# One sum with the shared expert in front, in place of two sums joined at the end

## What is computed

```python
scores = sigmoid(x @ router_w.T)                      # 4096 tokens, 16 experts
_, topk_idx = top_k(scores + e_bias, 4)
topk_w = take(scores, topk_idx) / sum                 # 4 experts for each token
...
for each expert: acc += combine[:, e] * ((silu(g) * u) @ d_w.T)    # I = 192, H = 512
shared = (silu(x @ shared_gate_w.T) * (x @ shared_up_w.T)) @ shared_down_w.T
return x2 + routed + shared
```

## Time and profile before

| | |
|---|---|
| median of 3 runs | 1870.16 us (1867.11 to 1880.34) |
| profiled execution, its own time | 1878.89 us |
| its span, first to last instruction | 1877.1 us |
| mean granted TensorE clock | 0.980 |
| busy, share of span | TensorE 95%, VectorE 61%, GpSimd 49%, ScalarE 47% |

### The profile page before, as it was taken

The page is one execution under the profiler, slowest core; times in us unless marked ns, Lnnn a source line. Parts: engine busy times, 40 slices in busy tenths (PEclk is TensorE's granted clock), DMA queues, the critical chain, the costliest instruction groups (busy, mean ns, idle before and its releaser), DMA issues. The chain is left out here.

```text
span 1877.1 us, 35163 instructions
## 1 busy us (share of the span) xinstructions
PE 1784.7 (95%) x8536; PEld 901.2 (48%) x8537; DVE 1145.0 (61%) x2171; ACT 880.2 (47%) x1726; POOL 924.6 (49%) x1127
## 2 busy tenths in 40 slices
PE   6799999999999999999999889899999999999995
PEld 5444454444454444544433345455555555555542
DVE  5567778787878787787788726433343333343433
ACT  2257766776676767667776642122211222211210
POOL 3424546676676667666555356033333333333341
PEclk9799999999999999999999989999999999999998
DMA  5422325344344534453345279898898888898889
GB/s 192 117 75 54 87 81 154 93 115 139 103 119 124 156 99 107 129 143 85 105 136 168 99 236 352 255 198 154 160 168 161 157 159 158 161 167 159 163 178 254
DMA packets 255899, 277.76 MB, mean 148 GB/s; under 512 B 57889, under 2 KB 184097, under 8 KB 253025
## 3 DMA queue, kind: packets, MB, share of 16 engines
q0 software_dynamic: 40880, 106.96, 27.1%
q1 hardware_dynamic: 151600, 127.10, 25.3%
q10 hardware_dynamic: 63296, 42.24, 8.3%
HBM read 145.65 MB, written 135.74 MB: 150 GB/s over the span
## 5 line engine op out<-in xcount | busy, mean ns | idle before, releaser
L995 DVE TENSOR_REDUCE mx<-ps_max 128x2 f32<-128x1024 f32 x512 | 618.3, 1220 | 175.3 <-PE ps_max L1205 160.5
L734 ACT ACTIVATE prob<-ps_exp 128x512 f32<-128x512 f32 x992 | 567.5, 598 | 147.9 <-PE ps_exp L1219 129.9
L1977 PE MATMUL ps_gu<-wts_sb,xT 128*128 x1152 | 399.4, 490 | 1.3 <-issue 1.3
L1219 PE MATMUL ps_exp<-qs,ks 98*128 98x512 bf16 x992 | 379.2, 383 | 19.0 <-ACT prob L734 16.6
L1205 PE MATMUL ps_max<-ks,qs 96*128 96x512 bf16 x1024 | 309.5, 384 | 10.7 <-DMA ks<-qk_parts 6.1
L1728 ACT ACTIVATE gs<-ps_gu 128x192 f32<-128x192 f32 x176 | 58.4, 332 | 520.1 <-PE ps_gu L1977 258.4
L1977 PEld LDWEIGHTS ps_gu<-wts_sb,xT 128*128 128x128 f32 x1152 | 209.7, 190 | 161.6 <-issue 46.5
L1676 POOL DMA_INDIRECT out<-yt,idx x72 | 111.7, 1551 | 355.5 <-ACT yt L1738 272.7
L1247 PE MATMUL ps_pv<-prob,vs 128*32 128x512 f32 x2048 | 252.8, 607 | 2.9 <-issue 2.9
L1219 PEld LDWEIGHTS ps_exp<-qs,ks 98*128 98x128 bf16 x992 | 96.7, 97 | 195.2 <-ACT prob L734 82.4
L1886 DVE SCALAR_TENSOR_TENSOR hid<-ps_gu,wsel,gs 128x192 f32<-128x192 f32 (+2 forms) x216 | 68.4, 345 | 173.4 <-ACT gs L1728 133.1
(11 more groups left out here) (196 smaller groups left out, 1997.6 us busy)
## 6 DMA issues: line engine op xcount, KB each, us to landing
xt<-rows_by_expert SPq DMA_DIRECT2D x296, 64.0 KB
dnr_sb<-in_dnr SPq DMA_DIRECT2D x144, 128.0 KB
xt<-rows_by_expert ACTq DMA_DIRECT2D x280, 64.0 KB
qk_parts<-parts POOLq DMA_DIRECT2D x112, 120.0 KB, 3.7
qs<-qk_parts SPq DMA_DIRECT2D x64, 192.0 KB, 3.1
wts_sb<-in_wts ACTq DMA_DIRECT2D x12, 1024.0 KB, 8.2
x_sb<-in_x SPq DMA_DIRECT2D x16, 512.0 KB
qs<-qk_parts SPq DMA_DIRECT2D x64, 128.0 KB, 3.2
```

The lines of the kernel that those rows point to most:

```text
L734: act.activation(prob[:, s, q], ps_exp[:, q % 2], ACT.Exp, scale=SCALE).then_inc(s_exp, 1)
L995: dve.tensor_reduce(mx[:, k % 2, 4 * s + 2 * p:4 * s + 2 * p + 2], ps_max[:, p], AX_X, ALU.max).then_inc(s_maxd, 1)
L1219: pe.matmul(ps_exp[:, q % 2], ks[0:ROWS + MROWS, kk, s * P:(s + 1) * P], qs[0:ROWS + MROWS, kk, q], start=True, stop=True).then_inc(s_sc, 1)
L1977: mm = pe.matmul(ps_gu[:, i, 0:2 * I], xT[:, i, d], w, start=(d == 0), stop=(d == DC - 1))
```

## The change

All sixteen shared pairs come first (`H0 = 16`), the 72 routed pairs end the kernel. There is one sum, the output. For shared tiles SyncE loads the x2 rows from the output into `yt` (`load_sum_rows`, in odd bodies, for two pairs), VectorE adds y to them in place (`y_sum`) and ScalarE stores them back. The copies of shared y by ScalarE, the second sum, its clears, the joins, the loads of both sums and the late pairs are gone. GpSimd's routed scatters all add to the output; tile 0s and tile 1s of pairs are still two chains, and each scatter also waits for the other chain up to a number from a new table, `tab[.., 2]`: the tiles of that chain that come before the first tile of this tile's expert (tokens of one expert are distinct). For an empty tile the number is that of all tiles before it. Both chains start with a clear of half of the rows behind the output. The last two routed pairs are finished one by one (`together`). Weights are loaded in later bodies, and the pads are written three to a body in bodies 5 to 8.

```diff
-        def clear_sums():
-
-            wait(s_zero, 1)
-            wait(s_w, 16 * 5)
-            late = SUM[1][EARLY * P:T].rearrange("(t p) d -> p t d", p=P)
-            pool.dma_start(late, zero[:, 0:D].unsqueeze(1).to_broadcast([P, T // P - EARLY, D])).then_inc(s_clear, 16)
-            for to in range(2):
-                pool.dma_start(SUM[to][T:T + P], zero[:, 0:D]).then_inc(s_clear, 16)
...
-    LATE = NT - EARLY
-    H0 = EARLY // 2
+    H0 = NT // 2
...
-            self.exists = not known or 0 <= h < H2
-            self.kind = SHARED if known and not H0 <= h < H1 else ROUTED
-            self.late = known and h >= H1
-            self.both = known and h > H1
+            self.exists = not known or 0 <= h < H1
+            self.kind = SHARED if known and h < H0 else ROUTED
             self.j = [(h - H0) * 2 + i for i in range(2)] if self.kind == ROUTED else None
-            self.t = None if self.kind == ROUTED else [(h if h < H0 else h - (H1 - H0)) * 2 + i for i in range(2)]
+            self.t = None if self.kind == ROUTED else [h * 2 + i for i in range(2)]
             self.routed = h - H0
...
-            self.together = not known or h < H1
+            self.together = not known or h < H1 - 2
...
-    WEIGHTS_AT = {0: 2, 1: 3, 2: 4, 4: 5, 8: 6, H0 + 3: 7}
+    WEIGHTS_AT = {0: 2, 2: 3, 5: 4, 8: 5, 11: 6, H0 + 3: 7}
...
+        def load_sum_rows(pair):
+
+            for s, n in done["x2_of"][pair.h]:
+                wait(s, n)
+            for i in range(2):
+                after(wait, s_yst[pair.slot(i)], 16 * pair.q)
+                sp.dma_start(yt[:, pair.slot(i)], rows_of(SUM, pair.t[i])).then_inc(s_yl[pair.slot(i)], 16)
...
+            if pair.kind == SHARED and pair.par == 1:
+                for ready in (before, pair):
+                    load_sum_rows(ready)
...
-            for n in range(2):
+            for n in range(4):
                 if is_at(pair, 5 + n):
-                    for e in range(POOL_PADS + 6 * n, POOL_PADS + 6 * n + 6):
+                    for e in range(POOL_PADS + 3 * n, POOL_PADS + 3 * n + 3):
...
-        wait(s_y, 2 * end.h + 1)
-        sp.dma_start(rows_of(SUM[0], end.t[0]), late_y(end, 0)).then_inc(s_last, 16)
-
-        wait(s_join[1], 16 * (EARLY // 2))
         for i in range(2):
-            wait(s_lst[i], 16)
-        sp.wait_ge(s_last, LATE_STORES)
+            wait(s_add[i], 16 * (NR // 2) + 16)
...
-        all_of("x2_stored", "cleared")
+        all_of("x2_stored")
...
+        wait(s_tab, 1)
+
+        for i in range(2):
+            rows = slice(T + i * P // 2, T + (i + 1) * P // 2)
+            pool.dma_start(SUM[rows], zero[0:P // 2, 0:D]).then_inc(s_add[i], 16)
 
         def add_rows(pair):
 
             wait(s_idx, pair.routed + 1)
             for i in range(2):
+                other = pool.value_load(tab[0:1, 2, bass.ds(pair.j[i], 1)], min_val=16, max_val=16 * (NR // 2) + 16)
                 wait(s_y, 2 * pair.h + i + 1)
 
-                after(wait, s_add[i], 16 * pair.routed)
+                wait(s_add[i], 16 * pair.routed + 16)
+                wait(s_add[1 - i], other)
                 at = idx[:, pair.slot(i):pair.slot(i) + 1]
-                pool.indirect_dma_start(SUM[i], bass.IndirectOffsetOnAxis(ap=at, axis=0), yt[:, pair.slot(i)], None,
+                pool.indirect_dma_start(SUM, bass.IndirectOffsetOnAxis(ap=at, axis=0), yt[:, pair.slot(i)], None,
                                         compute_op=ALU.add).then_inc(s_add[i], 16)
...
-        for i in range(2):
-            wait(s_add[i], 16 * (NR // 2))
-
-        def join(t, s):
-
-            rows = slice(t * P, (t + 2) * P)
-            pool.dma_start(SUM[0][rows], SUM[1][rows], accum_op=ALU.add,
-                           max_dma_last_dim=8192).then_inc(s, 16)
-
-        def load_sums(n):
-            t = EARLY + 2 * n
-            for o in range(2):
-                rows = SUM[o][t * P:(t + 2) * P].rearrange("(t p) d -> p t d", p=P)
-                pool.dma_start(sums[:, (LATE // 2) * o + n], rows).then_inc(s_sl[n], 16)
-
-        def add_first_late(pair):
-            wait(s_join[0], 16)
-            for i in range(2):
-                wait(s_y, 2 * pair.h + i + 1)
-                pool.dma_start(rows_of(SUM[0], pair.t[i]), late_y(pair, i), accum_op=ALU.add).then_inc(s_lst[i], 16)
-
-        wait(s_yp, H1)
-        load_sums(1)
-        join(EARLY, s_join[0])
-        load_sums(2)
-        early = iter(range(0, EARLY, 2))
-        for n in range(3, LATE // 2):
-            for t in (next(early), next(early)):
...
+        add_rows(Pair(H1 - 1, (H1 - 1) // 2, (H1 - 1) % 2))
...
-                    act.wait_ge(s_add[i], 16 * (pair.routed - 1))
+                    act.wait_ge(s_add[i], 16 * pair.routed)
...
-                if not ready.both:
+                if ready.kind == SHARED:
+                    store(ready)
+                else:
                     y_out(ready)
-            for ready in whole(before):
-                if ready.kind == SHARED and not ready.late:
-                    store(ready)
-            if before.both:
-                store_late(before)
...
+            step(dve.tensor_scalar(jt[:, 6], jt[:, 1], float(sizes(T)[0] // P), None, ALU.mult))
+            step(dve.scalar_tensor_tensor(jt[:, 6], jt[:, 3], -1.0 / P, jt[:, 6], ALU.mult, ALU.add))
+
+            step(dve.tensor_tensor(jt[:, 6], jt[:, 6], jrow[:, 0], ALU.subtract))
+            step(dve.tensor_tensor(jt[:, 6], jt[:, 6], jt[:, 2], ALU.mult))
+            step(dve.tensor_tensor(jt[:, 6], jt[:, 6], jrow[:, 0], ALU.add))
+
+            by_parity = [jt[:, k].rearrange("p (m i) -> p m i", i=2) for k in (6, 7)]
+            for i in range(2):
+                step(dve.tensor_scalar(by_parity[1].bitcast(I32)[:, :, i], by_parity[0][:, :, i], float(2 + i), None, ALU.add))
+            step(dve.tensor_scalar(jt[:, 7].bitcast(I32), jt[:, 7].bitcast(I32), 1, None, ALU.logical_shift_right))
+            step(dve.tensor_scalar(tab[0:1, 2].bitcast(I32), jt[0:1, 7].bitcast(I32), 4, None, ALU.logical_shift_left))
...
-                after(dve.wait_ge, s_add[i], 16 * (pair.routed - 1))
+                after(dve.wait_ge, s_add[i], 16 * pair.routed)
...
-        def both_sums(pair):
-            n = pair.h - H1
-            dve.wait_ge(s_sl[n], 32)
-            dve.tensor_tensor(sums[:, n], sums[:, n], sums[:, LATE // 2 + n], ALU.add).then_inc(s_both, 1)
-
         def y_sum(pair):
-            n = pair.h - H1
             dve.wait_ge(s_yp, pair.h + 1)
-            dve.wait_ge(s_both, n)
             for i in range(2):
-                dve.tensor_tensor(late_y(pair, i), y_of(pair, i), sums[:, n, i], ALU.add).then_inc(s_y, 1)
+                dve.wait_ge(s_yl[pair.slot(i)], 16 * pair.q + 16)
+                dve.tensor_tensor(yt[:, pair.slot(i)], y_of(pair, i), yt[:, pair.slot(i)], ALU.add).then_inc(s_y, 1)
...
+            for ready in whole(before):
+                if ready.kind == SHARED:
+                    y_sum(ready)
```

More of the change, by code:

```diff
@@ L44 @@
 IR = I - P
-EARLY = 20
 PARTS = 3
@@ L1347, in attention @@
             "memory_read": [(s_amp, MEM * NU)], "shared_weights": [(s_ws, 48)], "o_added": [(s_x2, 2 * NU)],
+            "x2_of": [[(s_x2st, 16 * c + 16)] for c in range(NU)],
             "xn2_early": [(s_xn2st[r], 16 * ((NU - 1 - r) // 2)) for r in range(2)]}
@@ L1403, in feed_forward @@
     wts_flat = wts_sb[:, :, :].rearrange("p e n -> p (e n)")
-    sums = wts_flat.rearrange("p (n t d) -> p n t d", t=2, d=D)
-    room = wts_flat[:, (E - 2) * W:(E - 2) * W + NR * (E + 9)]
+    room = wts_flat[:, (E - 2) * W:(E - 2) * W + NR * (E + 11)]
     big = room[:, 0:NR * E].rearrange("p (j e) -> p j e", e=E)
     jrow = room[:, NR * E:NR * (E + 3)].rearrange("p (k j) -> p k j", k=3)
-    jt = room[:, NR * (E + 3):NR * (E + 9)].rearrange("p (k j) -> p k j", k=6)
+    jt = room[:, NR * (E + 3):NR * (E + 11)].rearrange("p (k j) -> p k j", k=8)
     ps_y = own.enter_context(nc.psum_tensor("ps_y", [P, 4, D], F32))
@@ L1436, in feed_forward @@
     s_idx = sem("f_tokens")
+    s_yl = [sem(f"f_sum_rows_loaded{r}") for r in range(4)]
     s_yst = [sem(f"f_y_stored{r}") for r in range(4)]
     s_add = [sem(f"f_y_added{i}") for i in range(2)]
-    s_join = [sem(f"f_second_sum_added_{n}") for n in ("late", "early")]
-    s_sl = [sem(f"f_sums_loaded{n}") for n in range(LATE // 2)]
-    s_both = sem("f_both_sums")
-    s_lst = [sem(f"f_late_y_added{i}") for i in range(2)]
-    s_last = sem("f_last_y_stored")
     s_spg = sem("f_sp_gate")
@@ L1486, in pairs @@
                 body(*around(r * 2 + (L0 + i), r + L0 // 2, i))
-        for h in range(L1, H2):
+        for h in range(L1, H1):
             body(*around(h, h // 2, h % 2))
@@ L1517, in rows_of @@
         return dram[bass.ds(t * P, P)]
-    def late_y(pair, i):
-        return sums[:, pair.h - H1, i] if pair.both else yt[:, pair.slot(i)]
-    LATE_STORES = 16 * 2 * (LATE // 2 - 1)
     def after(eng_wait, s, n):
@@ L1576, in body @@
```

(37 more changed lines are left out.)

14 lines of the change are left out of this document (2 added, 12 removed).

## The result

The changed kernel takes 1897.81 us (median of 4 runs, 1889.98 to 1904.37) against 1875.25 of the kernel before in the same comparison (4 runs, 1867.11 to 1881.81): ratio 1.0117, 95% interval 1.0082 to 1.0153. That is slower, and 0.8 us above the range of the prediction. The median lies 17.2 us above the forecast of 1880.6: 5.1 of these are the base, since the kernel before has 1875.25 here and had 1870.16 when the forecast was made, and 12.1 are the change, 22.6 us where 10.4 were forecast. The profiled execution took 1900.96 us, span 1899.1, clock 0.978: 22.1 more than the profiled one before.

What follows compares the result with a forecast made beforehand. TensorE was taken to bound the routed stage, but not the front, parts of the shared stage or the tail. Terms -5.5 + 6.3 + 4 + 5.6 = +10.4 us gave profile 1889, median 1880.6, range 1866 to 1897.

Steps and rivals of the forecast that it cites:

- Part 2: Routed stage, scatters where experts begin, by the first tile's place (number modulo 4) in its burst: +4 us (+1 to +10).
- place 1: Experts beginning at a burst's second tile: late scatter delays idx copy and hT, 0.3 to 1.8 us each, +4 for four.
- places 2 and 3: Experts beginning at a burst's third or fourth tile: later scatters, hidden because VectorE's idx copy has slack before hT; 0.
- Part 1: Tail: nine empty tiles make one serial scatter chain, ending 30 us beyond TensorE; +5.6 us (+3 to +9).
- Parts 3 and 4: Shared stage, VectorE additions, larger table and loads: +6.3 us (-3 to +14); front without zeros: -5.5 (-8 to 0).
- The front's -5.5: Front: without GpSimd's 3.5 MB of zeros SyncE's store lands sooner, TensorE idles less, nearly all lasting; -5.5 us.
- body 4: Shared stage: VectorE's additions stand before most of its small operations, so hT is late; +2.5 us.
- body 7: Shared stage: nine more small table operations on VectorE make hT late; +1.8 us.
- the xT wait: Shared stage, TensorE's 4.9 us wait at 1179.90: more bytes ahead of the awaited tile; +2 us (-7 to +9).
- The DMA rival: Shared stage: sum rows land late, stalling VectorE 3 to 5 us in each of three groups; total +23, 1893; chance 0.22.
- A little faster: Spread pads remove the wait at 1179.90 and place 1 costs nothing: -3 us, 1868; chance 0.13.
- The table does what it says: Answers a rival: table off, every tile waits for the one before, +220 us, 2090; chance 0.02.

Runs made afterwards that it cites:

- Experiment 1: Changed kernel with idx holding token numbers of four pairs instead of two, all scatter waits kept: 1881.07 us, ratio 1.0024 to the kernel before.
- Experiments 2: Changed kernel with a second, never joined sum array for the second chain: without waits on the other chain 1879.6 us, with all waits 1900.74 us.
- experiment 3: Changed kernel with odd empty tiles adding to their own 128 spare rows and all empty tiles given the first one's table number: 1881.69 us, ratio 1.0000.
- experiment 6: Changed kernel with 3.5 MB of zeros written in the front to unread rows: 1887.77 us once, then 1903.20 beside 1902.85 for the unaltered changed kernel.

## Why the prediction was wrong

The sign was right, and so was the place: the waits between the chains, in the stage and in the tail, make +9.6 of the +10.4 us forecast and +21.0 of the +22.1 measured. Their size was not. By its own steps:

**Part 2, where experts begin, is the step that failed: +4 forecast (range +1 to +10), +12.9 measured.** The placing held: the second scatter is late in the bursts of tiles 29, 81, 109 and 121, the third in those of 14 and 38, the fourth in those of 35, 67, 71 and 103, and place 0 shows nothing. Read off the two-body periods above 16.53, place 1 cost 2.0, 2.4, 0.7 and 1.4 us, 6.5 for 4 forecast. The real fault is "hidden" for places 2 and 3: one or two periods behind their bursts TensorE's are longer by 1.0, 1.5, 0.5, 1.0 and 1.0, 5.0 us for 0, and in four of these five its weight loads wait 0.5 to 1.1 us for the down weights. I checked whether hT would be in time behind VectorE's idx copy, and it is; I did not follow the token copy, which stands behind the same wait, to SyncE and the down weights that it loads, though I had named it among what is queued there. The start of the stage, where the kernel before loses 1.5 us too, gave 1.2 more. Experiment 1 shows the cause: with the wait of the idx copy gone, the stage is back at 573.1.

**Part 1, the tail: +5.6 forecast, +8.1 measured.** Mechanism and count right (nine steps, tile 135 waits for 134). From tile 132 to the end 62.9 us went by for 60.4 in the sum. The 2.5 are spread: 0.4 from 132 to 134 (6.04 for 5.65), 0.65 from 134 to 135 (6.25 for 5.6), 0.9 in the eight steps behind (5.56 each for 5.44 in the sum), 0.6 behind the last issue. The estimate with the figure of the Trainium skill (DMA: Bandwidth & Descriptors, section Anatomy of one DMA), 4.9 a step, would have made nine steps 6.7 us too short; the trace, with 5.64, does not agree with it. Experiments 2 and 3 confirm that the empty tiles' chain makes the tail long: without it the tail is 19.3 and 20.5 us shorter, more than the whole forecast.

**Parts 3 and 4 together: +0.8 forecast, +1.1 measured, but by errors that cancel.** The front's -5.5 is -6.0 at the first staged matmul, and of the 5.1 us of experiment 6 only 1.1 are left at the shared stage and 0.35 in the medians: the claim that "nearly all should last" is not borne out. In the pair of profiles behind the table the shared stage does begin 6.7 us earlier, but the clock's sum of experiment 6 is 4.4 us smaller there too (18.7 against 23.1), 2.7 of them behind 940 us, long after the zeros, so these 6.7 can't all be put down to the zeros. In the shared stage the excess over 144.0 was 7.7 in this profile and 3.5 to 9.6 in others of the same stage; the terms are not mine: body 4 took 0.5 for +2.5 (up to 3.0 in other profiles), body 7 only 0.2 here for +1.8 (up to 3.7 in others), the xT wait moved into hT in body 6, and body 2 lost 4.1 to GpSimd's xn, which no term had. That last gap goes with the granted clock at the start of the stage. In six profiles the clock of the first 12 us is 1.00 (the upper level, 2.4 GHz, throughout), the first 24 matmuls take 7.98 us, and TensorE then waits for xn: 4.0 to 5.1 us in five, 1.1 in one. In the other seven, the kernel before among them, that clock is 0.79 to 0.88 (partly the lower level, 1.2 GHz), the 24 matmuls take 9.4 to 10.5, and there is no such gap. In the 12 us before the stage TensorE was busy for 8.8 us in all of the six, and in the seven for 5.4 to 6.7 us in five and 8.8 in two. Why the wait is longer than the 1.4 to 2.5 us that the full clock gains stays open.

**The rivals.** The DMA rival gave nearly the right time (1893) for a wrong reason: TensorE does not idle in every second shared body. The loads do cost 4.8 us, about what one of its three groups was priced at. "A little faster" needed place 1 to cost nothing, and it cost 6.5. The table does what it says.

## What to carry to other kernels

When a semaphore wait becomes longer, list everything behind each in-order engine that shares it, and follow each item to its last reader: the copy that I had checked was in time, the one behind it fed another engine's loads. A bookkeeping copy with a buffer two deep can make a hot engine wait for an old transfer; room for two more pairs bought 14 us here. And a dependency table has to be read for its padding too: nine empty tiles, each given its own number, made a serial chain of 50 us out of work that nobody needs, and another number with a second set of spare rows took 20.5 us off it.

## What was not expected of the hardware

A scatter of 256 KB that adds to HBM takes 4.6 to 5.5 us from its start to its landing in the tail above, with a DMA share of 0.42 between 1850 and 1890, and the next issue of the waiting GpSimd comes 0.8 us after the landing. Two chains side by side nearly doubled the rate (one scatter in 2.9 us from tile 137 to 143 in experiment 3, against 5.64), and the DMA moved 107 GB/s between 1856 and 1880 there, against 60 in the tail of one chain, so latency and not bandwidth was the price. And 3.5 MB of zeros on GpSimd's queue made a 120 KB store on SyncE's queue land in 10.9 us instead of 2.6, at a cost of 0.35 us between the medians in the end, which is within the noise.
